# fp16 bias terms, stationary causal values, a second activation and new orders in a two-layer audio tower

## The reference

```
comb = zeros(n, e).at[arange(n)[:, None], top2_idx].add(top2_prob)   # layer 0: gates
o    = einsum('enh,ehd->end', h, W2) + b2[:, None, :]
y    = einsum('ne,end->nd', comb, o)
...
attn = softmax(where(causal, scores, min), axis=-1)                  # layer 1
y    = (attn @ v) @ Wo
hid  = gelu(einsum('bnd,edf->bnef', y, W1) + b1)
out  = einsum('bned,bne->bnd', einsum('bnef,efd->bned', hid, W2) + b2, gate)
```

## Time and profile before

| | us |
|---|---|
| median of 3 runs | 4183.73 (4181.23 to 4189.27) |
| the profiled execution, its own time | 4183.28 |
| its span, first to last instruction | 4181.6 |

### The profile page before, as it was taken

One profiled execution on the slowest core, in us unless ns is written; L12 is line 12 of the kernel. 1 busy time (PEld: TensorE's weight loads), 2 busy tenths in 40 slices (PEclk: granted clock), 3 DMA queues, 4 the chain that ended last, 5 costly groups with the idle time before them and its releaser, 6 DMA issues.

```text
span 4181.6 us, 104776 instructions
## 1 busy us (share of the span) xinstructions
PE 3994.9 (96%) x41344; PEld 3003.6 (72%) x41344; DVE 3258.6 (78%) x8879; ACT 2767.7 (66%) x4797; POOL 2531.2 (61%) x2494
## 2 busy tenths in 40 slices
PE   9589999999999999999999999999999999999988
PEld 4256777777777777777777777777777777777766
DVE  4367887878888777888878888878878887887866
ACT  4236776766767666677776767776676777667654
POOL 2136666666666666666666666666666666666656
PEclk9679999999999999999999999999999999999999
DMA  6100100010110000111000011100111110010100
GB/s 184 40 28 29 31 27 23 16 31 29 31 31 27 21 20 29 31 31 31 19 22 26 29 31 31 31 19 18 30 29 31 31 31 19 17 31 29 29 16 7
DMA packets 137083, 127.62 MB, mean 31 GB/s; under 512 B 28944, under 2 KB 135376, under 8 KB 136592
## 3 DMA queue, kind: packets, MB, share of 16 engines
q1 hardware_dynamic: 136592, 120.91, 9.9%
HBM read 71.05 MB, written 49.55 MB: 29 GB/s over the span
## 4 chain that ended last, share of the span: by engine, by line
PE 80%; DVE 7%; ACT 6%; issue 3%; DMA 2%; SPq 1%; POOL 1%; ACTq 0%; DVEq 0%; POOLq 0%
PE pf L1313 14%; PE pf L1315 13%; PE pf L1314 13%; PE pa L1574 8%; PE pa L1313 4%; PE pa L1315 4%; PE pa L1314 4%; PE pa L1359 3%; PE pa L1460 3%; PE pa L1556 3%; PE pa L1422 2%; PE pa L1446 2%; PE pa L1654 2%; DVE h L1297 2%; ACT hid L902 2%
## 5 line engine op out<-in xcount | busy, mean ns | idle before, releaser
L680 POOL TENSOR_TENSOR hid_lo<-hid,hid_hi 128x504 f16<-128x504 f32 x1536 | 1793.0, 1177 | 1132.3 <-DVE hid_hi L1278 1132.2
L902 ACT ACTIVATE hid<-pf,vec 128x504 f32<-128x504 f32 x1536 | 1017.2, 679 | 469.7 <-PE pf L1315 377.1
L1313 PE MATMUL pf<-w_hi,hid_hi 128*126 128x128 f16 x6144 | 1129.5, 223 | 9.4 <-DVE h L1297 6.5
L1315 PE MATMUL pf<-w_hi,hid_lo 128*126 128x128 f16 x6144 | 1115.0, 221 | 0.0
L1314 PE MATMUL pf<-w_lo,hid_hi 128*126 128x128 f16 x6144 | 1114.7, 221 | 0.0
L1313 PEld LDWEIGHTS pf<-w_hi,hid_hi 128*126 128x126 f16 x6144 | 843.2, 137 | 136.4 <-DVE h L1297 60.7
L1314 PEld LDWEIGHTS pf<-w_lo,hid_hi 128*126 128x126 f16 x6144 | 844.4, 137 | 31.1
L1315 PEld LDWEIGHTS pf<-w_hi,hid_lo 128*126 128x126 f16 x6144 | 845.8, 138 | 0.0
L1278 DVE CAST hid_hi<-hid 128x504 f16<-128x504 f32 x1536 | 774.3, 523 | 35.2 <-ACT hid L902 26.6
L1297 DVE SCALAR_TENSOR_TENSOR h<-pf,gates,h 126x128 f32<-126x128 f32 x2048 | 572.9, 341 | 112.3 <-PE pf L1315 109.4
L1313 PE MATMUL pf<-xf_hi,w_hi 128*128 128x504 f16 x1536 | 581.8, 379 | 21.6 <-ACT hid L902 20.3
(11 more groups left out here) (208 smaller groups left out, 7401.7 us busy)
## 6 DMA issues: line engine op xcount, KB each, us to landing
qk_spread<-terms SPq DMA_DIRECT2D x224, 126.0 KB, 2.5
qk_spread<-terms SPq DMA_DIRECT2D x192, 63.0 KB, 2.3
y_scratch<-hid SPq DMA_DIRECT2D x32, 252.0 KB, 2.1
y_in<-y_scratch SPq DMA_DIRECT2D x32, 252.0 KB, 3.2
terms<-qk_hi SPq DMA_DIRECT2D x32, 252.0 KB, 2.4
terms<-qk_lo SPq DMA_DIRECT2D x32, 252.0 KB, 2.4
qk_spread<-terms SPq DMA_DIRECT2D x32, 252.0 KB
terms<-ot_hi SPq DMA_DIRECT2D x32, 252.0 KB, 2.4
```

The costliest lines, as they stand in the source:

```text
L680: nc.gpsimd.tensor_tensor(hid_lo[:, c % 8], hid[:, c % HIDS], hid_hi[:, c % 8], ALU.subtract).then_inc(hid_lo_done[c % 2], 1)
L902: nc.scalar.activation(hid[:, c % HIDS], pf[:, c % 2, 0:TOK], func, bias=vec[:, bias:bias + 1]).then_inc(F["hid_ready"], 1)
L1313: nc.tensor.matmul(out, ah, bh, start=start, stop=False, skip_group_check=skip)
L1315: return nc.tensor.matmul(out, al, bh, start=False, stop=stop, skip_group_check=skip)
```

## The change

1. **Second activation.** For odd chunks ScalarE runs the GELU twice from the same bank, first into hid_hi (fp16), then into hid. VectorE's cast stays for even chunks alone (`hid_hi_even`), and GpSimd waits for hid_ready at odd ones.
2. **fp16 bias terms.** The gates are split into terms (hi, hi, lo), b2 into (hi, lo, hi), 32 partitions each, so one fp16 matmul gives all three products. b2 has 12 DMAs, GpSimd splits it once (`split_bias2`), VectorE splits the gates each time (`split_gates`, two instructions), and the gate transpose is an fp16 product with ident16. TensorE waits for b2 only before the first bias product.
3. **Stationary causal values.** The probabilities are divided by their sums before they are transposed (8 VectorE instructions in place of one), the values are the stationary operand (64 columns, each head to its half of the output partitions), and the result is already transposed: 8 matmuls a pair, and one `turn` (four transposes) goes.
4. **Own orders.** Each engine's strings hold only its own steps; empty steps are gone, several steps are split, and all 15 strings are new. SP, GpSimd, ScalarE and VectorE skip the mixture steps in which they have nothing to do.
5. **Unused products.** PE_START has 189 letters "w"; each is one fp16 matmul of 504 columns into bank 2 of pf, whose result nothing reads. At a "w" after an expert's output it first waits until that bank was evicted.

In PE_ROUND the steps of the causal attention now stand as: k and q turned, A:bias2, h, scores 0 and 1, o o, scores 2 and 3, z's turn, o o, transposes 0, h h o h o, transposes 1, h h, transposes 2, values of sequence 0, o h, transposes 3, o h, values of sequence 1.

```diff
@@ the chunk, ScalarE @@
                 act.wait_ge(hid_lo_done[c % 2], n(half + (c - HIDS) // 2 + 1))
+                if c % 2 == 1:
+                    nc.scalar.activation(hid_hi[:, c % 8], pf[:, c % 2, 0:TOK], func, bias=vec[:, bias:bias + 1])
                 nc.scalar.activation(hid[:, c % HIDS], pf[:, c % 2, 0:TOK], func,
                                      bias=vec[:, bias:bias + 1]).then_inc(F["hid_ready"], 1)
...
@@ the chunk, GpSimd @@
-                if c % 2 == 1 or POOL_EVEN:
-
-                    pool.wait_ge(F["hid_hi_done"], n(before + c + 1))
+                if c % 2 == 0:
+                    pool.wait_ge(F["hid_hi_even"], n((before + c) // 2 + 1))
+                else:
+                    pool.wait_ge(F["hid_ready"], n(before + c + 1))
...
@@ bias terms @@
+            def split_bias2():
+
+                pool.wait_ge(small_loaded, 32 + 16 * TILES * BIAS_TERMS)
+                nc.gpsimd.tensor_copy(b2_terms[:], b2[:]).then_inc(b2_split, 1)
+                pool.wait_ge(b2_split, 1)
+                low = slice(TILES * EXPERTS, 2 * TILES * EXPERTS)
+                nc.gpsimd.tensor_tensor(b2_terms[low], b2[low], b2_terms[low], ALU.subtract).then_inc(b2_split, 1)
+                pool.wait_ge(b2_split, 2)
...
+            def split_gates(a, p):
+
+                S = SS[a]
+                dve.wait_ge(S["gate_made"], n(p + 1))
+                nc.vector.tensor_copy(gate_terms[0:TILE, a, 0:64].rearrange("p (s c) -> p s c", s=2),
+                                      gates_all[0:TILE, a].unsqueeze(1).to_broadcast([TILE, 2, TILES * EXPERTS])
+                                      ).then_inc(S["gate_hi"], 1)
+                dve.wait_ge(S["gate_hi"], n(p + 1))
+                nc.vector.tensor_tensor(gate_terms[0:TILE, a, 64:96], gates_all[0:TILE, a], gate_terms[0:TILE, a, 0:32],
+                                        ALU.subtract).then_inc(S["gate_ready"], 1)
...
-            for i in range(TILES):
-                sp.dma_start(b2[i * EXPERTS:(i + 1) * EXPERTS, :, i], b2_dram).then_inc(small_loaded, 16)
+            for term in range(BIAS_TERMS):
+                for i in range(TILES):
+                    first = (term * TILES + i) * EXPERTS
+                    sp.dma_start(b2[first:first + EXPERTS, :, i], b2_dram).then_inc(small_loaded, 16)
...
-            pe.wait_ge(small_loaded, 32 + 16 * TILES)
+            pe.wait_ge(small_loaded, 32)
...
@@ causal values, VectorE @@
+                for b in range(2):
+
+                    dve.wait_ge(S1["p2_ready"], n(p * 4 + 2 * b + 2))
+                    nc.vector.reciprocal(inv_sum[0:TILE, 4 * b:4 * b + 4],
+                                         row_sum[0:TILE, 2 * b:2 * b + 2].rearrange("p t h -> p (t h)")
+                                         ).then_inc(S1["rs_rec"], 1)
+                    dve.wait_ge(S1["rs_rec"], n(p * 2 + b + 1))
+                    for hd in range(HEADS2):
+                        i = 2 * b + hd
+                        for qt, c in halves:
+                            at = 4 * b + 2 * qt + hd
+                            last = nc.vector.tensor_scalar(p2[i][0:TILE, c], p2[i][0:TILE, c],
+                                                           inv_sum[0:TILE, at:at + 1], None, ALU.mult)
+                        last.then_inc(S1["p2_scaled"], 1)
+                    yield
...
@@ causal values, TensorE @@
+                def causal_values(b):
+
+
+                    pe.wait_ge(S1["p2t_ready"], n(p * 4 + 2 * b + 2))
+                    for kt, first, width in ((0, 0, SEQ), (1, TILE, TILE)):
+                        for hd in range(HEADS2):
                             c0 = 2 * D + hd * HEAD2
+                            last = nc.tensor.matmul(pa1[head_rows(hd), TURN, b * SEQ + first:b * SEQ + first + width],
+                                                    qkv[0:TILE, 2 * b + kt, c0:c0 + HEAD2],
+                                                    fs1[0:TILE, hd, kt * SEQ:kt * SEQ + width], start=(kt == 0),
+                                                    stop=(kt == 1), skip_group_check=True)
+                    last.then_inc(S1["turned"] if b else S1["pv2_done"], 1)
...
-                pe.wait_ge(S1["o2_ready"], n(p + 1))
-                turn(1, p * 7 + 6, xn[1])
...
@@ unused products @@
+            def unused():
+
+
+                evicted = 0
+                for i, part in enumerate(PE_START):
+                    if part != "w":
+                        continue
+                    experts = PE_START[:i].count("o") // CHUNKS0
+                    if experts > evicted:
+                        pe.wait_ge(F["gated"], n(experts))
+                        evicted = experts
+                    nc.tensor.matmul(pf[:, 2, 0:TOK], W("up1", 0, 128)[0], W("up1", 0, TOK)[0], start=True, stop=True)
+                    yield
```

More of the change, by code:

```diff
@@ L1 @@
 from contextlib import ExitStack, contextmanager
-from itertools import chain
+from itertools import chain, repeat
 import numpy as np
@@ L32 @@
 BAND, BAND_WIDTH = 5, 131
-POOL_EVEN = True
 HIDS = 4
@@ L216, in chunks_of, with each @@
+PE_ROUND = ("aohhaohaohaolhaollaohlaohllhaohhlaahaahoaoaohalaaloalllaalloolllhhlolhhlllaollaaallhhloolaolalhl"
+            "lholalhlhahoohoolhhooollallohaohoohhhahollahloolqoolhhoholhhllohlohloqolhqqoohhloohhqolohlh")
+PE_END = ("oohlollhohlhllhholhoohohhhllhllllloollhllloolllhlloolllolhollhllllhlhhholoohollllhhohoohohlllolo"
+          "oollhllllholoohhohhlhooohlolhhhohhoohohhoohhoohhoohhoohhoohhohohhoohhoohhoooohoooo")
 def chunks_of(kind, p):
     return [(kind, p, c) for c in range(EXPERTS * (CHUNKS0, CHUNKS1)[kind])]
-def each(work, chunks):
+def each(work, chunks, takes):
@@ L222, in each, with every_chunk, no_chunk, even_chunk @@
     for chunk in chunks:
-        work(*chunk)
-        yield
+        if takes(*chunk):
+            work(*chunk)
+            yield
+def every_chunk(kind, p, c):
+    return True
+def no_chunk(kind, p, c):
+    return False
+def even_chunk(kind, p, c):
+    return c % 2 == 0
+def last_of_expert(kind, p, c):
+    per = (CHUNKS0, CHUNKS1)[kind]
+    return c % per == per - 1
+def last_of_pair(kind, p, c):
+    return kind == 1 and c == EXPERTS * CHUNKS1 - 1
 def in_order(order, parts):
@@ L231, in in_order, with run_rounds, up, down @@
             next(parts[part])
-def run_rounds(queries_and_keys, first_attention, second_attention, hidden, output, orders):
+def run_rounds(queries_and_keys, first_attention, second_attention, hidden, output, orders,
+               hidden_of=every_chunk, output_of=every_chunk, unused=None):
+    def up(chunks):
+        return each(hidden, chunks, hidden_of)
+    def down(chunks):
+        return each(output, chunks, output_of)
     start, middle, end = orders
```

512 lines of the change are left out of this document (217 added, 295 removed).

## The result

| | before | after |
|---|---|---|
| median | 4183.35 us (4 runs, 4181.23 to 4189.27) | **4131.43 us** (4 runs, 4129.92 to 4133.53) |
| ratio to before | | **0.9874** (0.9857 to 0.9891) |
| span of the profiled execution | 4181.6 us | 4128.6 us |
| mean granted TensorE clock | 0.984 | 0.996 |

The kernel is faster by 1.3%: the direction of the forecast, and less than half of its size. The forecast had 117 us and 52 came; its range ended at 4131 us, and the median lies 0.4 us above that.

What follows compares the result with a forecast made beforehand. TensorE, busy 96%, was taken as the bound. Savings of 92 us in 30 rounds, 20 in the start and 5 in the end, sum 117, took 4183.3 to 4066 us (chance 0.60); range 3990 to 4131.

Steps and rivals of the forecast that it cites:

- rival 1: Causal values: the halves do not overlap or the tiling change drains TensorE, so nothing is saved there; 4093 us, chance 0.12.
- the sum of the work: TensorE's work in a round: bias terms, gate transposes, xn's turn and causal values together save 2.7 us, 119.3 to 116.6.
- Waits in a round: TensorE's idle time in a round: 3.05 us, less 1.85 freed, plus 1.5 new, makes 2.7 us.
- the GELU's and the small ones about as now: TensorE's remaining waits in a round, for GELUs (0.6 us before) and small causes, were taken to stay unchanged.
- The new wait: TensorE's transposes of causal probabilities wait for VectorE's masks, maxima and normalization: about 1.5 us a round.
- the three old waits: TensorE's waits for ScalarE's probability copies, k2t copy and shifted queries: up to 0.8, 0.75 and 0.3 us a round freed.
- Rival 2: The new wait at the transposes is covered and a round's waits fall to 1.0 us; 4015 us, chance 0.11.
- ScalarE: 24 more activations and one table load fewer raise its work to 97.8 us a round, 82%, leaving room on average.
- The start: Before the rounds: unused products hold TensorE's clock up; 20 us saved, including 2 from no longer waiting for b2's DMAs.
- Rival 4: In the start, unused products do not hold the clock and only block: +5 instead of -20; 4091 us, chance 0.08.
- The end: After the rounds: one linear stage less (2 us) and some waits, 5 us saved.
- my own tests: Signs of being wrong: rounds under 118 or over 121 us, or GELU waits passing 60 us in all.

Runs made afterwards that it cites:

- run 8: Changed kernel, but TensorE waits for both exponentials before the first of a pair of layer-0 scores: 4135.57 us.
- Run 4: Kernel before with only the fp16 bias terms (part 2 of the change), in the old orders: 4173.09 us, ratio 0.9974.
- run 1: Changed kernel without the activation that writes the high half of odd chunks, after pair 0: 4141.22 us.
- run 5: Changed kernel without the reciprocals and scalings that normalize the causal probabilities, after pair 0: 4121.18 us.
- run 7: Changed kernel with the first transposes of probabilities moved behind the two hidden steps that followed them: 4132.06 us.
- run 13: Changed kernel with TensorE's order of run 7 and VectorE's cast of an even chunk moved ahead of the third and fourth masks: 4137.21 us.
- run 12: Kernel of run 9 without GpSimd's subtraction for low halves after pair 0: 4109.32 us, 120.67 us a round.
- run 10: Changed kernel without GpSimd's subtraction for the low half of every hidden chunk, after pair 0: 4108.98 us, 120.64 us a round.
- Run 11: Changed kernel without the second activations, the normalization and GpSimd's low-half subtraction, all after pair 0: 4072.66 us, 119.50 us a round.
- run 3: Changed kernel without the 189 unused products: 4156.48 us.
- run 9: Changed kernel with TensorE's order of run 7 and VectorE's cast of an even chunk moved ahead of the first scaling: 4202.35 us.
- run 6: Changed kernel without VectorE's casts of even chunks after pair 0, which only signal: 4175.26 us.

## Why the prediction was wrong

**The prices of the work were right.** A group of four bias products took 0.39 us, first to last record:

```profile
1150.91 0.39 PE L1392 MATMUL pa<-b_terms,gate_t 128*126 128x128 f16 x4
```

Now count each record of TensorE from its start to the next record's start, without the visible idle time between; so counted, all records add up to the busy time. Over the rounds the causal values went from 2.55 to 1.58 us a round (-0.97, forecast -0.85), the bias products from 1.76 to 0.51 (-1.25, forecast -1.30), the gate turns from 0.37 to 0.12 (-0.25, forecast -0.10) and the turns of xn from 2.75 to 2.21 (-0.54, forecast -0.45). That is 3.0 us off, for 2.7; the 0.3 more are late starts that stood behind the old ones (0.12 us behind one group of values a round, for instance).

The halves overlap: a sequence's eight records take 0.86 us, forecast 0.8, and rival 1 falls. But a change of tiling has a price. Where nothing is waited for, the first record behind a change starts 0.09 us later than usual, here 0.31 us behind the record ahead of it for 0.21:

```profile
1654.56 0.38 PE L1325 MATMUL pf<-xf_hi,w_lo 128*128 128x504 f16 x1
1654.87 0.86 PE L1653 MATMUL pa<-fs,v 126*64 126x252 f32 x8
```

Of the four changes that the new values bring, the two at their ends are in the 1.58 us; the two ahead of them, 0.19 us, stand in the records before and come off the gain. What the Trainium skill (TensorEngine Tiling, Key Properties) says, that changing the tiling mode drains TensorE, agrees with the trace, at about half of the 0.17 us that the prediction had tried for one change. (Four changes at 0.17 would have left 0.17 of the 0.85, not 0.15.)

**The first step that failed is the sum of the work**, "-2.7 us a round": it took prices for busy time. The work went, 3.0 us of it, and busy time fell by 1.6. In the count above the third products of the hidden steps took 1.26 us more (10.65 to 11.91), layer 0's scores 0.82 more (5.78 to 6.60), the first products of the output steps 0.36 and z's turn 0.21, while all others together took 1.2 less. None of these had more work. A record of 504 columns lasts 0.38 us and its successor usually starts 0.21 behind it, so one that starts up to 0.17 us late leaves TensorE busy all the same:

```profile
1183.19 0.38 PE L1325 MATMUL pf<-xf_hi,w_lo 128*128 128x504 f16 x1
1183.62 0.44 PE L1392 MATMUL pa<-b_terms,gate_t 128*126 128x128 f16 x4
```

These bias products start 0.44 us behind the record ahead of them, 0.23 late; 0.17 of it counts as busy, and the 0.06 left are too short for the lists of waits. Of the 1.26 us, 0.44 only moved there from output steps, with the layer-0 scores that now follow hidden steps; most of the rest is this kind of late start. The scores of layer 0 wait one by one (run 8). For the first products of the output steps no cause was looked for. So much of the missing busy time is waiting too, in short pieces, and I had forgotten that the new PE_ROUND changes what stands behind what.

**The second is "Waits in a round", and above all the clause "the GELU's and the small ones about as now".** The new wait was forecast well, 1.37 us against 1.5, at the place and behind the engine that I named, and the three old waits went as said. Rival 2, waits of 1.0 us, falls all the more. The sum was still wrong: GELUs +0.46 us, evictions +0.48 (before's list of the same stretch has none), low halves +0.21 and xn +0.18. I had treated TensorE as a bound from which work can be taken one for one, because it was 96% busy. Run 4 shows it in the old orders already: 0.93 us less busy time, 0.62 us more waiting. Runs 1, 5, 7, 8 and 13, and run 12 beside run 10, each take one wait or one piece of work away and get 0.3 us or nothing; the largest single gain, run 10, is 0.8 from 47 us of GpSimd's work. Run 11 gets 1.9 from three together. That single reliefs are handed on is shown by these runs; that the reason is several in-order chains through VectorE, ScalarE and GpSimd, each within some 2 us of the round, is my reading of them. Which chain would be last with all reliefs made was not tried.

**ScalarE** was forecast at 97.8 us a round and has 2903.8 / 30 = 96.8; the second activations are not what holds the rounds (run 1). Table loads fell by one a round as forecast (404 to 374 in all), though from 13 to 12, where I counted 14 to 13. Where ScalarE's input is ready, nothing stands behind a load; the median gap over all 374 is 0.01 us:

```profile
551.83 1.28 ACT L905 ACT_TABLE_LOAD   x1
553.12 0.68 ACT L905 ACTIVATE hid<-pf,vec 128x504 f32<-128x504 f32 x1
```

The 1.38 us of drain that the Trainium skill (ScalarE: Activation LUTs, What ACT_TABLE_LOAD costs) adds would end the load of 551.83 at 554.5, but the GELU began at 553.12: the trace does not agree, and the measurement decides.

**The start** gave 26.7 us for 20. Rival 4 falls: the unused products are worth 20.1 us of it (run 3), inside the bounds of nothing and 35. In the other 6.6 us is b2's wait: in the changed kernel z's turn begins at 132.85 instead of 134.44. Part 2 alone shortens the start by 5.2 us (run 4), but that is about the scatter of a start, so how the rest divides stays open. That the start came out beyond -20, the middle of two bounds, is no merit of the sum. **The end** got 1.2 us longer, not 5 shorter, at a granted clock of 0.94 instead of 0.96; it was not taken apart either.

Of my own tests, that rounds are not over 121 us failed by 0.4; GELU waits were to stay under 60 us in all and have 34.9.

## What to carry to other kernels

An engine that is busy for 96% is a bound only until its next wait, and part of its busy time can be short waits that overlapping records hide: compare starts with starts. Before counting work taken from it as time, go through the waits behind that work and ask how much later their releasers could be; where they are not early, the gain is handed on, and one relief is worth little until the others are made too. Before an instruction of VectorE is moved, look at what GpSimd does at the new place, and at how long TensorE will then stand.

## What the runs showed of the hardware

**GpSimd's subtraction holds up VectorE, by kind of instruction.** Beside two subtractions of GpSimd (two SBUF inputs, 1.1 us each) four of VectorE's fp32 scalings in SBUF took 2.79 us instead of 1.00 (run 9). In the changed kernel, where one ran beside them, casts of 128x504 took 854 ns in the mean instead of 430 (235 and 533 of them), and a 126x32 subtraction of two SBUF tensors 826 instead of 193. Masks (one input in PSUM) and maxima (one input), two of them, kept 0.54 and 0.61 us. The Trainium skill (SBUF — State Buffer, Who interferes with whom) calls it an exclusive lock on a shared port pair, not a sharing of bandwidth, and its GPSIMD Engine Reference (Key points) names the instructions that need it: those in a two-port mode or with two SBUF inputs. The trace agrees: the durations grow by about what is left of the subtraction. It probably slows run 6 as well: without casts GpSimd's subtractions moved, two of the first four scalings are stretched in all of its 30 rounds (2.78 us for the four, at 554.91), and the wait behind them grew from 39.6 to 65.3 us. The granted clock fell in 17 of its rounds too. No run takes the subtraction out of that kernel, so this is not shown.

**A hole of some 3 us in TensorE's work cost up to as much again, and not every time.** In run 9, 16 of 30 rounds have a mean granted clock of 0.97 to 0.99 and last 124.2 to 126.2 us; the others show 1.00 and 121.8 to 123.1, with the same wait of 2.21 us in the same place. What decides between them these runs do not show. The changed kernel, whose longest waits are 1.4 us, shows 1.00 in all of its rounds. In the start the same effect runs the other way: with products that nobody reads the granted clock over 125 to 365 us is 0.97 instead of 0.74, and the start 20 us shorter.

**A change of tiling costs 0.09 us.** In both kernels, wherever TensorE goes from the whole array to halves, quarters or row groups without a wait, the next record starts 0.31 us after the one ahead of it instead of 0.21 (where that has 504 fp16 columns), or 0.15 instead of 0.06 (128 columns), in nearly every case. Back from the halves of the causal values it is 0.20 instead of the 0.11 of an fp32 product of 126 columns.
